# Four tiles of the first product opened by halves, and half of the first x turned on TensorE ahead of the first fold

## The reference, cut to what matters

```python
x_filtered = ifft(fft(x_quat, axis=1) * spectral_gate, axis=1).real
x_rotated  = hamilton(q_left_n, hamilton(x_filtered, q_right_conj))
probs = softmax(xf @ Wr.T)
h = gelu(xf @ W1[7] + b1[7])            # 256 -> 1024, exact gelu
y = (h @ W2[7] + b2[7]) * probs[:, 7:8] # 1024 -> 256
out = x + y
```

## Time and profile before

| | us |
|---|---|
| median of 3 runs | 107.39 |
| lowest and highest of the 3 | 106.76, 109.37 |
| the profiled execution's own time | 106.51 |
| its span, first to last instruction | 104.7 |

### The profile page before, as it was taken

How to read it: one execution, slowest core, us unless ns; L and a number is a source line. 1 busy time by engine, 2 the same in 40 slices (tenths; PEclk the granted TensorE clock), 3 DMA queues, 4 the chain that set the end, 5 groups by cost and what they waited for, 6 DMA issues and landing times.

```text
span 104.7 us, 1512 instructions
## 1 busy us (share of the span) xinstructions
PE 100.3 (96%) x568; PEld 85.2 (81%) x568; DVE 67.1 (64%) x145; ACT 50.2 (48%) x83; POOL 25.6 (24%) x16
## 2 busy tenths in 40 slices
PE   7897999999999999999999999999999999999990
PEld 7687988878888878888888888878888878888980
DVE  1579779969255899389223997272394972379451
ACT  1467795464440494484434444844434444441700
POOL 3300000009999500000000000059999000000000
PEclk9999999999999999999999999999999999999999
DMA  3999990052002314260500050000006040000005
GB/s 72 309 277 352 230 129 0 9 130 67 0 0 66 138 36 171 62 138 3 178 22 0 0 207 0 0 0 0 0 0 200 6 200 0 0 0 0 0 5 195
DMA packets 10870, 8.38 MB, mean 80 GB/s; under 512 B 7920, under 2 KB 8816, under 8 KB 10864
## 3 DMA queue, kind: packets, MB, share of 16 engines
q1 hardware_dynamic: 10144, 7.51, 25.8%
q10 hardware_dynamic: 720, 0.79, 2.5%
HBM read 6.20 MB, written 2.10 MB: 79 GB/s over the span
## 4 chain that ended last, share of the span: by engine, by line
PE 91%; DMA 2%; DVE 2%; ACT 1%; DVEq 0%; issue 0%
PE pre L681 40%; PE acc L688 25%; PE acc L696 14%; PE pre L651 2%; DMA quats<-in_small 2%; PE acc L603 2%; PE lT_bank L640 2%; PE acc L692 1%; PE acc L690 1%; PE acc L622 1%; DVE y L510 1%; PE extra L622 1%; PE lT_bank L622 1%; ACT xT_hi L310 1%; ACT w_hi L326 1%; PE extra L613 0%
## 5 line engine op out<-in xcount | busy, mean ns | idle before, releaser
L338 ACT ACTIVATE h_hi<-pre,quats 128x512 fp32r<-128x512 f32 x32 | 22.1, 690 | 43.6 <-PE pre L681 41.9
L476 DVE TENSOR_TENSOR h_lo<-h_all,h_hi 128x512 fp32r<-128x512 f32 x32 | 21.8, 688 | 20.5 <-ACT h_all L340 20.2
L688 PE MATMUL acc<-w_parts,h_hi 128*128 128x512 f32 x116 | 32.3, 391 | 0.0
L688 PEld LDWEIGHTS acc<-w_parts,h_hi 128*128 128x128 f32 x116 | 21.5, 188 | 4.4
L681 PE MATMUL pre<-xT_hi,w_hi 128*128 128x512 f32 x60 | 24.0, 400 | 0.0
L681 PE MATMUL pre<-xT_lo,w_hi 128*128 128x512 f32 x60 | 23.6, 394 | 0.0
L696 PE MATMUL acc<-w_parts,h_lo 128*128 128x256 f32 x128 | 23.0, 282 | 0.0
L285 POOL TENSOR_TENSOR exps<-e_const,shifted 128x32 f32<-128x32 f32 x4 | 22.3, 5580 | 0.2
L696 PEld LDWEIGHTS acc<-w_parts,h_lo 128*128 128x128 f32 x128 | 20.0, 189 | 2.7 <-DVE h_lo L476 0.7
L340 ACT ACTIVATE h_all<-pre,quats 128x512 f32<-128x512 f32 x32 | 21.8, 683 | 0.0
L681 PE MATMUL pre<-xT_hi,w_lo 128*128 128x512 f32 x60 | 18.7, 392 | 0.0
(11 more groups left out here) (75 smaller groups left out, 61.4 us busy)
## 6 DMA issues: line engine op xcount, KB each, us to landing
x_sq<-in_x SPq DMA_DIRECT2D x12, 128.0 KB, 3.7
x_in<-in_x SPq DMA_DIRECT2D x3, 512.0 KB, 3.2
out<-y SPq DMA_DIRECT2D x3, 512.0 KB, 2.7
w<-in_W SPq DMA_DIRECT2D x4, 256.0 KB, 4.4
x_in<-in_x SPq DMA_DIRECT2D x2, 256.0 KB, 4.5
w_rest<-in_W_rest SPq DMA_DIRECT2D x2, 256.0 KB, 3.5
w_first<-in_W_first ACTq DMA_DIRECT2D x2, 132.0 KB, 2.9
x_sq<-in_x SPq DMA_DIRECT2D x4, 64.0 KB, 3.7
```

Source lines behind the costliest of these rows:

```text
L338: nc.scalar.activation(h_hi[:, s, :], pre[f % 2][:, :], ACT.Gelu, bias=b1_cols[:, f:f + 1]).then_inc(h_hi_ready, 1)
L476: nc.vector.tensor_tensor(h_lo[:, s, :], h_all[:, s, :], h_hi[:, s, :].bitcast(F32), ALU.subtract).then_inc(h_lo_ready, 1)
L688: nc.tensor.matmul(acc[j][:, :], rows, w2_parts[:, f, :, :], start=(f == 0), stop=False)
```

## The change

- Four tiles (f = 0 to 3) are opened by halves instead of two. Tiles 2 and 3 go to the banks `lT_bank` and `extra`. The opening is called as pair 0 half 0, pair 1 half 0, pair 0 half 1, then fold(2), fold(3), then pair 1 half 1. Pair 0 takes the product w_hi x_lo within each half now, so TensorE waits for x_lo of half 0 before it goes to pair 1.
- TensorE turns half 0 of the first x before the first fold. Both transposed channel halves lie in one bank, `acc[2]`; therefore ScalarE waits for all four transposes, VectorE for both x_high of half 0, and ScalarE's copies for both x_low.
- fold(2) and fold(3) write `acc[0]` and `acc[1]`, and wait until VectorE has read chunk 0 and the router from there.
- ScalarE's order is now: w1_high of chunk 0 for k = 0, x_high of half 0 (two), w1_high for k = 1, split_w1(1), x_high of half 1.
- VectorE's order is now: w1_low (two), take_router (two), its transposes, x_low of half 0, split_w1(1), x_low of half 1, split_w2(0).
- The second product of f = 0 waits at its first tile until all of W1 is split (VectorE has read `acc[0]`, `acc[1]` and `acc[3]`). The router waits for h of the third tile.

The core of the diff:

```diff
+    OPENING = 4
+        first_pre = pre + [lT_bank, extra]
-        xT_ps = [bank[:, 0:HALF] for bank in (acc[2], extra)]
+        xT_ps = [acc[2][:, k * HALF:(k + 1) * HALF] for k in range(KC)]
-        fold_banks = [None] + [... for bank in (acc[3], lT_bank, extra)]
+        fold_banks = [None] + [... for bank in (acc[3], acc[0], acc[1])]
...
# ScalarE
-                    act.wait_ge(first_x_turned, k + 1)
+                    act.wait_ge(first_x_turned, KC)
-            for k in range(KC):
-                first_w1_high(k)
+            first_w1_high(0)
             act.wait_ge(scale_ready, 1)
             for k in range(KC):
                 first_x_high(0, k)
+            first_w1_high(1)
             split_w1(1)
...
# VectorE
-                    dve.wait_ge(first_xT_hi_ready, KC * half + k + 1)
+                    dve.wait_ge(first_xT_hi_ready, KC if half == 0 else KC + k + 1)
             for k in range(KC):
                 first_w1_low(k)
-            turn_first_x()
-            first_x_low(0)
-            first_x_low(1)
-            split_w1(1)
             dve.wait_ge(wr_padded, 1)
             for k in range(KC):
                 take_router(k)
+            turn_first_x()
+            first_x_low(0)
+            split_w1(1)
+            first_x_low(1)
             split_w2(0)
...
# TensorE
-                if i == 3:
-                    pe.wait_ge(xT_copied, KC)
+                if i > 1:
+                    pe.wait_ge(w1_first_lo_ready, KC)
+                    pe.wait_ge(wr_ready, KC)
...
+            def opening(pair, half):
+                tiles = range(2 * pair, 2 * pair + 2)
+                if pair == 0:
+                    pe.wait_ge(w1_first_hi_ready, KC)
+                else:
+                    pe.wait_ge(w1_hi_ready, pair)
+                pe.wait_ge(first_xT_hi_ready, KC * (half + 1))
+                for f in tiles:
+                    products(w1_hi, xT_hi, f, starts=(half == 0))
+                if pair == 0:
+                    pe.wait_ge(w1_first_lo_ready, KC)
+                    for f in tiles:
+                        products(w1_lo, xT_hi, f)
+                    pe.wait_ge(first_xT_lo_ready, KC * (half + 1))
+                    for f in tiles:
+                        last = products(w1_hi, xT_lo, f, ends=(half == 1))
+                        ...
+                else:
+                    pe.wait_ge(first_xT_lo_ready, KC * (half + 1))
+                    for f in tiles:
+                        products(w1_hi, xT_lo, f)
+                    pe.wait_ge(w1_lo_ready, pair)
+                    for f in tiles:
+                        last = products(w1_lo, xT_hi, f, ends=(half == 1))
+                        ...
-                pe.wait_ge(h_ready, FT * b + f - 1)
+                pe.wait_ge(h_ready, FT * b + f - 1 if b > 0 or f >= OPENING + 2 else f - OPENING + 1)
...
+                    if f == 0 and b == 0 and j == 0:
+                        pe.wait_ge(w1_lo_ready, N_CHUNKS - 1)
                     if f == 0 and b == 0 and j == 2:
-                        pe.wait_ge(xT_copied, 1)
-                    if f == 0 and b == 0 and j == 3:
-                        pe.wait_ge(w1_lo_ready, 1)
+                        pe.wait_ge(xT_copied, KC)
...
-            first_fold()
-            turn_first_x()
-            fold(1)
-            opening()
-            for i in range(2, N_CHUNKS):
-                fold(i)
+            turn_first_x()
+            first_fold()
+            fold(1)
+            opening(0, 0)
+            opening(1, 0)
+            opening(0, 1)
+            fold(2)
+            fold(3)
+            opening(1, 1)
             for b in range(N_BLOCKS):
                 for f in range(FT):
-                    if b > 0 or f > 1:
+                    if b > 0 or f >= OPENING:
                         first_product(b, f)
```

More of the change, by code:

```diff
@@ L145, in adaln_ffn @@
         logitsT = lT_bank[:, 0:2 * P].rearrange("p (j t) -> p j t", j=2 * TT)
-        xT_ps = [bank[:, 0:HALF] for bank in (acc[2], extra)]
+        first_pre = pre + [lT_bank, extra]
+        xT_ps = [acc[2][:, k * HALF:(k + 1) * HALF] for k in range(KC)]
         first_fold_banks = [bank[:, 0:CHUNK] for bank in acc[:KC]]
         wr_ps = [bank[:, CHUNK:CHUNK + NE] for bank in acc[:KC]]
-        fold_banks = [None] + [bank[:, :].rearrange("p (k f) -> p k f", k=KC) for bank in (acc[3], lT_bank, extra)]
+        fold_banks = [None] + [bank[:, :].rearrange("p (k f) -> p k f", k=KC) for bank in (acc[3], acc[0], acc[1])]
         q_loaded = sem("q_loaded")
@@ L313, in copy_first_x @@
             def copy_first_x():
+                act.wait_ge(first_xT_lo_ready, KC)
                 for k in range(KC):
-                    act.wait_ge(first_xT_lo_ready, k + 1)
                     nc.scalar.activation(xT[0][:, k, 0:HALF], xT_ps[k], ACT.Copy).then_inc(xT_copied, 1)
@@ L337, in gelu @@
                 s = f % SLOTS
-                nc.scalar.activation(h_hi[:, s, :], pre[f % 2][:, :], ACT.Gelu,
+                bank = first_pre[f] if b == 0 and f < OPENING else pre[f % 2]
+                nc.scalar.activation(h_hi[:, s, :], bank[:, :], ACT.Gelu,
                                      bias=b1_cols[:, f:f + 1]).then_inc(h_hi_ready, 1)
-                nc.scalar.activation(h_all[:, s, :], pre[f % 2][:, :], ACT.Gelu,
+                nc.scalar.activation(h_all[:, s, :], bank[:, :], ACT.Gelu,
                                      bias=b1_cols[:, f:f + 1]).then_inc(h_ready, 1)
-            for k in range(KC):
-                first_w1_high(k)
+            first_w1_high(0)
             act.wait_ge(scale_ready, 1)
@@ L630, in router @@
                     pe.wait_ge(xT_copied, KC)
-                    pe.wait_ge(w1_lo_ready, 2)
+                    pe.wait_ge(h_ready, 3)
                 else:
@@ L643, in router, with products @@
                 last.then_inc(logitsT_done, 1)
-            def opening():
-                def products(w, part_of_x, half, f, ends=False):
-                    tokens = slice(half * HALF, (half + 1) * HALF)
+            def opening(pair, half):
+                tokens = slice(half * HALF, (half + 1) * HALF)
+                def products(w, part_of_x, f, starts=False, ends=False):
                     for k in range(KC):
-                        last = nc.tensor.matmul(pre[f][:, tokens], w[:, k, f * P:(f + 1) * P], part_of_x[0][:, k, tokens],
-                                                start=(w is w1_hi and part_of_x is xT_hi and half == 0 and k == 0),
+                        last = nc.tensor.matmul(first_pre[f][:, tokens], w[:, k, f * P:(f + 1) * P],
+                                                part_of_x[0][:, k, tokens], start=(starts and k == 0),
@@ L653, in products @@
                                                 stop=(ends and k == KC - 1), skip_group_check=True)
                     return last
[L656 to L659, removed]
-                        products(w1_hi, xT_hi, half, f)
-                    if half == 0:
-                        pe.wait_ge(w1_first_lo_ready, KC)
-                    for f in range(2):
-                        products(w1_lo, xT_hi, half, f)
@@ L665, in opening @@
-                for f in range(2):
-                    for half in range(2):
-                        pe.wait_ge(first_xT_lo_ready, KC * (half + 1))
-                        last = products(w1_hi, xT_lo, half, f, ends=(half == 1))
-                    last.then_inc(pre_done, 1)
+                tiles = range(2 * pair, 2 * pair + 2)
[4 more added lines that the diff above has]
+                pe.wait_ge(first_xT_hi_ready, KC * (half + 1))
@@ new lines, in opening @@
+                for f in tiles:
[7 more added lines that the diff above has]
+                        last = products(w1_hi, xT_lo, f, ends=(half == 1))
+                        if half == 1:
+                            last.then_inc(pre_done, 1)
+                else:
[5 more added lines that the diff above has]
+                        last = products(w1_lo, xT_hi, f, ends=(half == 1))
+                        if half == 1:
+                            last.then_inc(pre_done, 1)
```

## The result

| | kernel before | changed kernel |
|---|---|---|
| median of 22 runs, us | 106.34 | 107.78 |
| lowest run, us | 105.83 | 106.81 |
| profiled execution, us | 106.51 | 107.06 |
| its span, us | 104.7 | 105.3 |

The ratio is 1.013, with a 95% interval of 1.0109 to 1.015: the changed kernel is slower by 1.1 to 1.5%, within the 2% of the forecast and in its direction.

The account below looks back on a forecast made before the run. TensorE, 96% busy, was taken as the bound. 16.9 less 15.88 gave +1.0 us on the profiled 106.51, so 107.5; a third of the distance to the shifted median 108.4 made it 107.8 us, range 106.9 to 108.9.

Parts of the forecast that it names:

- What bounds it: TensorE, busy 96% of the span, never waits from 9.37 us on; better cover in the opening wins at most 0.5 us.
- the comparable moment: Start of the second product of f = 0 with tiles 0 to 3 done: 15.88 us before, 16.9 forecast.
- The mechanism: Transposes first delay the fold 1.19 us, then w_hi, w_low and x_low on VectorE; TensorE idles 1.45 us with pair 1 behind.
- The places: Forecast times in the changed profile: fold 5.2, w_hi for k = 1 7.4, x_low ending near 10.2, second product 16.9 us.
- The sum, +1.0: Start of the second product, 16.9 less the comparable 15.88 us: the whole opening 1.0 us slower.
- The new wait at the second product: TensorE, free at 16.75, waits for w_lo of chunk 3, done at 16.85 us: costs 0.1 us.
- The base: The profiled 106.51 us of the kernel before, 0.9 us faster than the median of the runs shown, 107.39.
- The clock as part of the spread between runs, swallowed by the changed kernel's idle time: Lower clock between 7 and 10.2 us cost the old chain half a us per us; now the 1.45 us idle swallows it.
- Rival B: TensorE's clock goes up late or falls in the stall: 109.3 us if low until 14, some 113 throughout the opening; 12%.
- Rival A: VectorE's chain is shorter, x_lo of half 0 is there at 8.8 and no stall comes: 106.0 to 106.9 us; 12%.
- Rival C: A hidden wait exceeds its cover, above all x_in landing later than 4.2: 108.3 to 109.3 us; 8%.
- Rival D: More than 2% faster, with no known mechanism, as only 0.5 us of idle time can be won; 4%.

Follow-up runs that it names:

- the last pair of runs: Four tiles by halves, orders of the kernel before, but x_low of half 0 ahead of VectorE's transposes: 0.9963; same with transposes ahead of the first fold: 1.004.
- The second profile: The changed kernel, unchanged, run again beside the first experiments: ratio 1.0121 to the kernel before, median 107.16 us, profiled execution 107.60 us.
- the warm-up controls: Seven warm-up matmuls instead of six, in the changed kernel (ratio 1.0129) and in the kernel before (ratio 1.0005).
- the router's run: The changed kernel with VectorE's two router operations moved behind x_low of half 1: ratio 1.0126 to the kernel before.
- the filling by folds: The changed kernel with w_hi x_hi of tiles 2 and 3, fold(2) and fold(3) ahead of TensorE's wait for x_lo of half 0: ratio 1.011.

## Why the prediction was right, and where it was not

- *What bounds it.* Right: from its restart on, TensorE runs without a gap in the kernel before, and in the changed one with none but the 0.24 us at the second product. No cover that the prediction counted behind that moment gave way. The span less the comparable moment is 88.8 and 88.9 in the kernel before (104.7 - 15.88; 104.1 - 15.16 with seven warm-up matmuls) and 89.0 in the changed one (105.3 - 16.27; 105.8 - 16.84).
- *The mechanism.* Right, link by link: fold behind the transposes, w_hi for k = 1 behind the x_high, w_low, router and transposes on VectorE ahead of x_low, TensorE stalled with ready work behind it in its list. That x_low's place on VectorE costs is shown by moving it ahead (1.0032 against 1.0121). ScalarE's link is seen in the waits of its profile, but its ratio (1.0096) is not clear of the noise. The swap's own cost is shown only in the last pair of runs, where the transposes on VectorE no longer hold TensorE up; alone in the kernel before it costs nothing measurable.
- *The places.* They were worked out for a clock that rises late, as in the profile of before. The second profile, with a clock nearer to that, has 5.05, 7.17, 9.94 and 16.84 for the forecast 5.2, 7.4, 10.2 and 16.9; the first has 4.93, 6.58, 9.37 and 16.27. The stall was 1.19 and 1.16 for 1.4. Part of that is two ways of counting: the prediction's 1.45 goes from where the last matmul's issue ends, the profile's idle time from its modelled end, as the 0.53 of before does, with which the prediction compares it. Counted from the issue the stall is 1.35 (7.96 + 0.12 to 9.42) and 1.32.
- *The sum, +1.0.* Measured 1.0 to 1.2 between like executions, 1.4 between the medians. Two terms were too small. The new wait at the second product: I had 0.1, and it is 0.24 (the last two half matmuls start at 15.79 and 15.91, so the second product could start at 16.03, and it comes at 16.27). The 1.52 us from the end of the folds to w_lo of chunk 3 held (12.88 + 1.73 = 14.61 to 16.12). What I had left out is the hand-over from w_lo to the matmul, 0.15 us (16.12 to 16.27); in the run where the profile names w_lo as the releaser it is 0.14 (16.90 + 1.28 = 18.18 to 18.32). And the first second product itself takes 0.1 more (16.27 to 17.28, against 14.49 to 15.40 before): its first matmul, behind the wait, is followed after 0.31 instead of 0.23.
- *The base.* I took the kernel before at the bound of its profile, restart at 9.37. In the execution with an early clock it restarts at 8.63 (the one with seven warm-up matmuls), and its median over 22 runs is 106.34, not 107.39. The forecast time of 107.8 came out right because a base of 106.51 that was near the true median, a sum that was up to 0.4 short, and an addition of 0.3 for the median of three runs went together; the last was a guess that three runs could not bear out. The mechanism is borne out by the runs; that the number meets 107.78 to 0.02 is luck.
- *The clock as part of the spread between runs, swallowed by the changed kernel's idle time.* Half right. The stall does swallow a low clock behind the fold (no wait at x_lo in the profiles with a clock low beyond 8 us), but the changed kernel's own chain up to x_lo runs through the first fold, and so it too is 0.5 us slower at a later clock (107.06 and 107.60).
- *Rival B*, a clock that rises late or falls in the stall: it did not fall, since the matmuls behind the stall of 1.19 us ran at the upper level, 0.12 each. That the idle time ahead of the transposes keeps it low the warm-up controls speak against. That the swap makes it rise later is not settled. Read from where the distances of TensorE's starts halve, it rises between 4.6 and 7.0 us in the four profiles without the swap, and between 4.7 and 9.8 in the ten with it, four times behind 8 us (one of them with x landing at 5.3). The latest is that of the router's run, whose first half matmuls still take 0.21 and more:

```profile
8.39 1.41 PE L660 MATMUL pre<-xT_hi,w_hi 128*128 128x256 f32 x4
9.60 0.70 PE L660 MATMUL pre<-xT_hi,w_lo 128*128 128x256 f32 x4
```

  The times of the last two runs fit it: 105.34 to 106.34 without the swap, 105.83 to 107.86 with it. So a part of what the swap costs may be the clock and not the order; no run separates the two. *Rival A* fell: the stall is there. *Rival C* shows up in single executions only: where the transposes started at 4.64, or once at 5.42, instead of about 4.2, the whole chain came later by as much. (In the chances, the 0.84 within 2% counts half of C, where the text says most of it.) *Rival D* had no mechanism and did not come.
- *The rule on transposes* (the Trainium skill, "TensorE: Matmul & The Clock Gate", Part 4: PE-mode transpose), by which transposes don't count as busy time: the first profile of the changed kernel does not bear out a later rise. Its four transposes took 0.66 us from the start of the first to the fold, less than the 0.86 of before, and the last two only 0.11 and 0.12, so the clock rose in them, with nothing but an idle 0.6 us and transposes since the warm-up. In the other profile of the same program it rose later, in the fold, so this is one execution against the rule and no more. The same page, Part 1, says that the moment varies from run to run for one kernel; that agrees.

## What to carry to other kernels

In a list worked out, more ready work covers a wait only if it stands ahead of the waiting instruction: four tiles gave nothing until x_lo no longer stood behind the transposes. When a step is moved on one engine, follow the operand through every other engine's list to the last one that needs it, and then look at what the next gate waits for, as the filling by folds showed. And compare two profiles only after checking that the clock rose at a like place in both.

## What was not expected of the hardware

The moment at which TensorE's clock rises differs between executions of one program, and with it the first fold: its four matmuls cost 0.9 us (4 x 0.22), 1.63 and 1.76 us in three executions of the same opening sequence (changed kernel twice, and the one with one more warm-up matmul at 5.03 to 6.79 us), against 1.89 in the kernel before, 0.13 of it start-up. The load of half 0 of x, 256 KB, issued ahead of the others of that size, landed after 2.8 to 3.1 us in most profiles of the swap, and let the transposes start at 4.1 to 4.4 us, but it took 3.3 and 4.1 us in two, where they started at 4.64 and 5.42.
